# Folded cross-attention on one core: another order of SyncE's transfers in each batch, and the first batch's softmax moved into the opening

## The reference, cut to what matters

```python
x = x + tanh(g_xattn[0]) * xattn(layernorm(x), ctx_768, Wq, Wk, Wv, Wout, bout)
x = x + tanh(g_ffn[0]) * ffn(layernorm(x), Wg, W1, W2, Ws1, Ws2)
# xattn: 8 heads of 64; softmax(q @ k.T * SCALE) @ v, then @ Wout + bout
# ffn: softmax gate over 16 experts, the best 2 of each token, plus a shared expert
```

## Time and profile before

| what | us |
| --- | --- |
| median of 3 runs | 997.63 (997.59 to 1003.64) |
| the profiled execution, its own time | 998.84 |
| its span, first to last instruction | 996.9 |
| PE busy in it | 879.4 (88%) |
| DVE, POOL, ACT busy | 770.3, 603.8, 517.4 |

### The profile page before, as it was taken

How to read it: one execution, slowest core, us unless ns; L and a number is a source line. 1 busy time by engine, 2 the same in 40 slices (tenths; PEclk the granted TensorE clock), 3 DMA queues, 4 the chain that set the end, 5 groups by cost and what they waited for, 6 DMA issues and landing times. The chain is left out here.

```text
span 996.9 us, 20482 instructions
## 1 busy us (share of the span) xinstructions
PE 879.4 (88%) x6332; PEld 815.3 (82%) x6332; DVE 770.3 (77%) x1871; ACT 517.4 (52%) x1188; POOL 603.8 (61%) x603
## 2 busy tenths in 40 slices
PE   7469999898998999887768999999869999999996
PEld 6358889798888888877756888888749999789996
DVE  6648889787888888877746898888847878468885
ACT  6437777676776767543215555554204444144442
POOL 3206767687676777666862455555434667536766
PEclk8588999999999999999997999999989999999998
DMA  8054555555555555667734344444249999488882
GB/s 231 21 158 124 173 181 183 162 175 170 177 183 160 162 184 177 207 188 216 220 124 151 128 167 164 160 164 165 92 162 299 341 344 343 151 277 271 263 276 89
DMA packets 140756, 188.96 MB, mean 190 GB/s; under 512 B 14822, under 2 KB 104810, under 8 KB 140656
## 3 DMA queue, kind: packets, MB, share of 16 engines
q1 hardware_dynamic: 125296, 145.45, 47.7%
q0 software_dynamic: 15360, 42.24, 11.0%
HBM read 107.86 MB, written 86.09 MB: 195 GB/s over the span
## 5 line engine op out<-in xcount | busy, mean ns | idle before, releaser
L778 POOL TENSOR_TENSOR prob<-prob,row_sum 128x616 f32<-128x616 f32 x64 | 77.9, 1217 | 137.1 <-DVE row_sum L1061 136.9
L1294 POOL DMA_INDIRECT rows_scratch<-row,slot x64 | 67.6, 1057 | 74.5 <-DVE row L1547 59.9
L1700 POOL DMA_INDIRECT rows_scratch<-prow x80 | 78.7, 984 | 49.9 <-issue 29.9
L79 PE MATMUL ps_s<-M_hi,xT_hi 128*128 128x308 f32 x256 | 84.8, 331 | 26.8 <-DVE prob L1051 26.7
L1700 POOL DMA_INDIRECT out<-prow x80 | 78.7, 983 | 48.8 <-issue 27.3
L79 PE MATMUL ps_h<-w_flat,eyT_hi 128*128 x320 | 96.5, 302 | 0.0
L1810 ACT ACTIVATE eyT_hi<-ps_ey 128x512 fp32r<-128x512 f32 x80 | 47.9, 598 | 91.9 <-PE ps_ey L1722 91.1
L80 PE MATMUL ps_o<-VW_lo,PT_hi 128*128 128x256 f32 (+1 forms) x320 | 90.6, 283 | 0.0
L80 PE MATMUL ps_h<-w_flat,eyT_hi 128*128 x320 | 89.7, 280 | 0.0
L81 PE MATMUL ps_h<-w_flat,eyT_lo 128*128 x320 | 89.6, 280 | 0.0
L953 ACT ACTIVATE prob<-prob,rstd 128x616 f32<-128x616 f32 x64 | 51.7, 808 | 57.1 <-DVE prob L1051 56.9
(11 more groups left out here) (350 smaller groups left out, 3423.1 us busy)
## 6 DMA issues: line engine op xcount, KB each, us to landing
prow<-rows_scratch SPq DMA_DIRECT2D x160, 258.0 KB, 3.7
vw_raw<-vw_scratch SPq DMA_DIRECT2D x32, 512.0 KB
vw_scratch<-stage SPq DMA_DIRECT2D x60, 154.0 KB
rows_scratch<-blank SPq DMA_DIRECT2D x34, 258.0 KB, 4.7
xT_raw<-in_xT SPq DMA_DIRECT2D x32, 256.0 KB, 4.8
x_tok<-in_x SPq DMA_DIRECT2D x32, 256.0 KB, 2.8
x_scratch<-x_tok SPq DMA_DIRECT2D x32, 256.0 KB, 2.5
row<-x_scratch SPq DMA_DIRECT2D x16, 512.0 KB, 3.9
```

The source lines that it names most:

```text
L79: nc.tensor.matmul(out, lh, rh, start=start and n == 0, stop=False)
L778: nc.gpsimd.tensor_tensor(pr, pr, row_sum[i][:, :].unsqueeze(2).broadcast_to((P, H, CK)), ALU.mult).then_inc(normed, 1)
L1294: pool.indirect_dma_start(c.rows1, bass.IndirectOffsetOnAxis(slot1[:, t:t + 1], 0), row[G % NX][:, i, :], None).then_inc(scattered[G % NX] ...
L1700: pool.indirect_dma_start(dram, bass.IndirectOffsetOnAxis(target, 0), row[u][:, i, 0:columns], None, bounds_check=bound, oob_is_err=False) ...
```

## The change

In SP's body the rows ahead are loaded one batch sooner (those of b + 1 in batch b, the very first ahead of the opening), x transposed and the context group follow, then the stores of parts 1 and 2, and only then the token rows and the packed rows of b. The blank stores come first as well. The scores, exponentials, sums and normalisation of batch 0 leave `body` and stand among the opening's parts, and the inverse deviations of the first two groups' tokens are worked out by POOL instead of DVE.

```diff
 def body (sync)
+                        if b + 1 < GB * (GROUPS - 2):
+                            wait(sp, ahead_stats, 2 * b)
+                            load_x_ahead(sp, c, a, b + 1, 1 - par)
+                        elif not exists(g + 2):
+                            if q == 0:
+                                sp.wait_ge(c.blank_made, 3)
+                            blank_ends(GB * (g - GROUPS + 2) + q)
+                        if not (last and q >= GB - 2):
+                            sp.wait_ge(a.x_split, b + 1)
+                            load_x_side(sp, c, a, b + 2, par)
+                        if q == 0 and exists(g + 2):
+                            sp.wait_ge(a.ctx_split, g + 2)
+                            load_group(sp, c, a, g + 2)
+                        if made_in(b - 1) or b == 0:
+                            store_part(b - 1 + AHEAD, 1)
+                            store_part(b - 1 + AHEAD, 2)
                         if b > 0:
                             wait(sp, x1_stats, 2 * (b - 1))
                             wait(sp, x1_out[par], 16 * (b // 2))
                             load_x(sp, c, a, b, par)
-                        if exists(g + 2):
-                            wait(sp, ahead_stats, 2 * (b - 1))
-                            load_x_ahead(sp, c, a, b, par)
-                        else:
...
-                        if q == 0 and exists(g + 2):
-                            sp.wait_ge(a.ctx_split, g + 2)
-                            load_group(sp, c, a, g + 2)
-                        if not (last and q >= GB - 2):
-                            sp.wait_ge(a.x_split, b + 1)
-                            load_x_side(sp, c, a, b + 2, par)
-                        if b > 0:
                             load_vw(b)
-                        if made_in(b - 1) or b == 0:
-                            store_part(b - 1 + AHEAD, 1)
-                            store_part(b - 1 + AHEAD, 2)
                         if n:
                             store_part(n, 0)
                         if b > 0:
                             store(b - 1, 1 - par)
+                load_x_ahead(sp, c, a, 0, 0)
                 for n in range(AHEAD):
...
 gpsimd: norm(b, 0) and norm(b, 1) in body only for b > 0, and ahead of groups(body)
+                rstd_by_newton(nc.gpsimd, linked(pool, first_chain, 0),
+                               a.stats1[:, 0:4 * GB * 6].rearrange("p (t s) -> p t s", s=6), c.rstd1[:, 0:4 * GB],
+                               var0[:, :], work0[:, :])
+                pool.sem_inc(rstd_ready, 1)
+                for i in range(2):
+                    norm(0, i)
 tensor: scores(b, g, q, 0) and scores(b, g, q, 1) in body only for b > 0, and ahead of the parts
+                pe.wait_ge(a.x_split, 1)
+                pe.wait_ge(a.M_lo, 2 * H)
+                scores(0, 0, 0, 0)
                 values(0)
+                values(1)
+                scores(0, 0, 0, 1)
                 for n in range(AHEAD):
-                    if n + 1 < AHEAD:
+                    if 0 < n < AHEAD - 1:
                         values(n + 1)
 scalar: exponentials(b, 0) and exponentials(b, 1) in body only for b > 0
+                        if b == 0:
+                            act.wait_ge(part_out[2], 2 * 32 * (3 * GB // 4))
...
+                    if n < 2:
+                        act.wait_ge(rstd_ready, 1)
+                        exponentials(0, n)
                 groups(body)
 vector: subtract_max and sums in body only for b > 0
-                rstd_by_newton(nc.vector, linked(v, first_chain, 0),
...
+                subtract_max(0, 0)
                 low_values(0)
+                low_values(1)
+                subtract_max(0, 1)
                 for n in range(AHEAD):
...
+                    if n < 2:
+                        sums(0, n)
                 groups(body)
```

More of the change, by code:

```diff
@@ L808, in body @@
                             split_group(nc.gpsimd, pool, a, g + 2)
-                        norm(b, 0)
+                        if b > 0:
+                            norm(b, 0)
                         if not (last and q == GB - 1):
@@ L813, in body @@
                             stats_ahead(g, q)
-                        norm(b, 1)
+                        if b > 0:
+                            norm(b, 1)
                         pool.wait_ge(a.x_in[par], 16 * (2 * g + q // 2 + 1))
@@ L904, in body @@
                             pe.wait_ge(a.M_lo, 2 * H * (g + 1))
-                        scores(b, g, q, 0)
+                        if b > 0:
+                            scores(b, g, q, 0)
                         if not last:
@@ L910, in body @@
                             project_part(b - 1 + AHEAD, 2)
-                        scores(b, g, q, 1)
+                        if b > 0:
+                            scores(b, g, q, 1)
                         if b > 0:
@@ L1009, in body @@
                             high_M_units(b, g, q, 0)
-                        if q == 0:
-                            act.wait_ge(rstd_ready, 1 if first else g)
-                        exponentials(b, 0)
+                        if q == 0 and not first:
+                            act.wait_ge(rstd_ready, g)
+                        if b > 0:
+                            exponentials(b, 0)
+                        if b == 0:
+                            act.wait_ge(part_out[2], 2 * 32 * (3 * GB // 4))
                         if made_in(b - 1) or b == 0:
@@ L1017, in body @@
                             mean_ahead(b, 2 * g + q // 2, q % 2)
-                        exponentials(b, 1)
+                        if b > 0:
+                            exponentials(b, 1)
                         if n:
@@ L1032, in _ @@
                 high_values(0)
+                high_values(1)
                 for n in range(AHEAD):
-                    if n + 1 < AHEAD:
+                    if 0 < n < AHEAD - 1:
                         high_values(n + 1)
@@ L1094, in body @@
                         n = made_in(b)
-                        subtract_max(b, 0)
+                        if b > 0:
+                            subtract_max(b, 0)
                         if not last:
                             low_M_units(b, g, q, 0)
-                        sums(b, 0)
-                        subtract_max(b, 1)
                         if b > 0:
+                            sums(b, 0)
+                            subtract_max(b, 1)
                             residual(b - 1, 0)
-                        sums(b, 1)
+                            sums(b, 1)
                         if n:
```

8 lines of the change are left out of this document (1 added, 7 removed).

## The result

The changed kernel takes 963.56 us (median; 961.82 to 973.45) against 997.61 us for the kernel before on the same chip: a ratio of 0.967, 95% interval 0.959 to 0.975. The forecast was 977.0 with a range of 966 to 992, so the change gained more than the range allowed. The profiled execution took 962.98 us, 35.86 us less than the one of before.

A forecast was written before the change was run, and what follows sets the result against it. In batches 2 to 26 a late store holds ACT, ACT holds DVE and DVE holds PE. Gains of 17.7 + 1.8 + 1.95 + 0.4 = 21.85 us off 998.84 gave 977.0, range 966 to 992.

The forecast's parts named there:

- the size of a batch without the stall: Batches 2 to 26: 13.25 us each once stores go ahead of packed rows, 331.25 in all, a gain of 17.7 us.
- the pair of batches 2 and 3 at 13.09: Batches 2 and 3 of the kernel before, 26.17 us together, taken as showing a batch without late stores.
- the allowance for context groups and later loads: Batches 2 to 26: 13.25 us taken instead of 13.09, for context groups split in one of four and later loads.
- batch 10 at 12.81: Rival for batches 2 to 26: every batch as short as batch 10, 12.81 us, gaining 28.7; total 966, chance 0.10.
- Rows ahead priced at 0: Batches 2 to 26: removing ACT's 27.8 us wait for rows ahead gains 0, bounds 0 to 2 us.
- the bound of 28.7 for the whole stage: Batches 2 to 26: upper bound of the gain from stores ahead of packed-row loads, 25 batches at 12.81 us.
- The chain store, ACT, DVE, PE: Batches 2 to 26: a late store holds ACT, ACT holds DVE, DVE holds PE; ACT waited 40.3 us for stores.
- the 2.8 us sooner of batch 8: Batch 8: the first part store goes at about 181.7 instead of 184.54, 2.8 us sooner in the new order.
- The cost of 0: Batches 2 to 26: packed-row loads now behind the stores go out 2.0 to 2.6 us later, at no cost.
- the cover of 2.4 us: Packed rows in a 13.25 us batch: they may come 2.4 to 2.5 us later before PE waits for their split.
- slower rival: Packed rows reach POOL's cast too late: with a flight of 7.1 us batches take 14.65, total 1012; chance 0.08.
- Last groups, opening: Batch 28 gains 1.8 us, batch 27 1.95; opening and batch 0 net 0.4, with 2.0 lost and 2.4 saved.

The follow-up runs named there:

- the rows ahead alone: Kernel before the change, with only the rows ahead loaded one batch sooner, first in SP's order; stores stay behind the packed rows: 983.08 us, ratio 0.981.
- the run with the loads first: Changed kernel with token-row and packed-row loads put back in front of the stores of parts 1 and 2: 969.39 us, ratio 0.969.
- the last run: Changed kernel, opening's store of batch 4's part 0 before batch 0's packed rows, and from batch 27 token and packed rows before the stores: 962.0 us, ratio 0.960.
- the order alone: Kernel before the change with SP's new order only, batch 0's softmax left in its batch: 965.85 us, ratio 0.963.

## Why the prediction was wrong, and where it was right

**The step that failed: the size of a batch without the stall.** The prediction took 13.25 us for a clean batch; it is 12.79, and 25 x 0.46 = 11.5 of the missing 14.0 us are that. Of the 0.46, 0.30 is its yardstick, the pair of batches 2 and 3 at 13.09, which was not clean: ACT waited 1.67 and 1.38 us for rows ahead in them. The kernel before, ACT and then the windows of the two batches:

```profile
101.04 0.42 ACT L961 ACTIVATE unused<-x_ahead 128x256 bf16<-128x256 f32 x1 [1.67 <-DMA x_ahead<-in_x]
...
113.98 0.42 ACT L961 ACTIVATE unused<-x_ahead 128x256 bf16<-128x256 f32 x1 [1.38 <-DMA x_ahead<-in_x]
```

```profile
93.84:107.07 13.23, 12.72 (x97) 12.14 (x95) 11.87 (x23) 9.82 (x26) 9.11 (x7) 1.00 0.58 178
107.07:120.01 12.94, 12.54 (x97) 12.09 (x95) 11.87 (x23) 9.48 (x26) 10.74 (x9) 1.00 0.59 179
```

At one for one beyond some 1.2 to 1.35 that is 0.3 to 0.5 and up to 0.2 of their excess of 0.44 and 0.15 over 12.79; their first copies of a part were not late. The other 0.16 was the allowance for context groups and later loads, and it was not needed: batches that load a context group last 12.76 to 12.81 in the changed kernel, and so do those that split one. The other yardstick that it had, batch 10 at 12.81, was the right one, and stood as a rival with a chance of 0.10. Its price, 966, still lay above the result, since batch 10 too is 0.02 slower than the mean, and the opening and the part behind the attention gave 2.7 us more than taken, 1.85 of them by chance as far as the spread of that part tells.

**Rows ahead priced at 0.** Wrong, and the same error seen from the other side. The mean wait of 27.8 / 22 = 1.26 us lies just at the free 1.2 to 1.35, so 9 of the 22 waits went beyond it. Batch by batch, the excess over 12.79 in the kernel before is the lateness of ACT's first copy of a part (25.0 us in sum over batches 2 to 26) plus what the rows-ahead wait exceeds 1.25 us by (3.5): together 28.5 of the 29.2 that went, and within 0.1 us in every batch but 25, where 0.3 is left. The bound of 2 us was too small, and the bound of 28.7 for the whole stage did not hold. The 14.7 us that the rows ahead alone gave are mostly not this wait: with their load out of the line the waits for stores fell by 13.0 as well.

**The chain store, ACT, DVE, PE: right.** All four waits fell as announced or further: stage stores 40.3 to no row (under 8 expected), kT to no row (under 10), PE's two 28.8 to 8.0 (about 12). The reason was read from batch 8, which loads a context group; there the stores came 2.3 us after the copies. In the batches up to 23 without a context group they came 0.05 to 0.8 us after, right behind the packed rows, so the 2.8 us sooner of batch 8 is not the usual case. There the gain is mostly the shorter flight, 4.9 us for 6.7, which the prediction had in words (the bytes ahead instead of behind) but gave no number. How much of it each load in front takes was not separated; the run with the loads first shows that token and packed rows in front cost the stores 1.0 us of flight, of which about 0.1 reaches a batch.

**The load behind the stores.** The cost of 0 was right, the cover of 2.4 us was not: 0.2 is left, so the 0 held by far less than was worked out. The load leaves 7.6 us into a batch instead of 4.7 to 5.4 in an unstalled batch without a context group, 2.2 to 2.9 later (2.0 to 2.6 were expected). For batch 8 the prediction took off its 4.4 us only what batch 9 would shrink by to 13.25. But the load is issued in batch 8, which shrank too, from 14.41 to 12.77; and the second scores, behind which PE wants the rows, stood 195.86 - 189.69 = 6.17 us into batch 9 and now stand 3.77 into a batch. That is 4.4 - 1.64 - 2.40 = 0.36, and the cast begins 0.2 later in batch 8 than before. That POOL would show under 0.6 us of cast waits per batch was right (13.8 / 25 = 0.55). Its slower rival needed a flight of 6.6 us; batch 8 took 5.5, the usual batch 6.0. By the rule of the Trainium skill (DMA: Bandwidth & Descriptors, "Why a DMA increments its semaphore by 16 and not by 1") it was estimated at 7.1; the trace does not bear this out, and no row here shows single engines.

**Last groups, opening.** Batch 27 gave 2.31 (1.95 expected); batch 28 gave 1.33 (1.8), because batch 27's packed rows stood behind stores that nobody waits for, which the last run removes. The first part product came at 45.51, 1.8 late (2.0), PE's next product 2.8 us behind the start of ACT's long-delayed copy instead of 4.9 (half was expected); and the wait for the store grew from 3.27 to 5.49. Batch 2 began 1.21 sooner (0.4), and by the halves of the change that is SyncE's order, not the softmax: the order alone gave 1.96.

## What to carry to other kernels

A yardstick for "without the stall" must be free of every other wait, so take the shortest stretch with the same work, or list the waits inside the one you take. A wait on an engine with slack is free only as far as the next thing would have been waited for anyway; compare the mean wait with that figure before pricing it at zero. On a queue issued in order, look first at what can be issued while the issuing engine would stand waiting: moving loads into that gap gave 26.6 of the 29.2 us with the largest load still in front of the stores. And a wait for a transfer has two parts, when it was issued and how long it flew; read both in several batches, not in the one with the largest wait.

## What the hardware showed that was not expected

The same 616 KB load took 6.0, 5.4 and 4.5 us when it was asked for 7.6, 8.3 and 9.6 us into a batch, so that asking 2 us later made it land only 0.7 later. The 256 KB of token rows leave just in front of it in all three; that it shares the way with them and with the stores is a reading, not shown, as no row tells the engines apart. The part behind the attention varied from 501.4 to 510.1 us between profiles with the same instructions there, more than any of the smaller edits moved the kernel.
